# A two-pass graph network kernel: the first stage of 24 of the dense edge groups made in pass 1, kept in a DRAM table and read back in pass 2

## The reference

```python
# layer 0
edge_input = concat([x[src], edge_attr])                 # 96 + 32
messages = gelu(edge_input @ mW1 + mb1) @ mW2 + mb2
gates = sigmoid(gelu(edge_input @ gW1 + gb1) @ gW2 + gb2)
aggregated = segment_sum(messages * gates, dst)
h = x + gelu(concat([x, aggregated]) @ uW1 + ub1) @ uW2 + ub2
x1 = layernorm(x + layernorm(h) * ln_g + ln_b)
# layer 1
deg = segment_sum(ew, dst) + 1
norm = rsqrt(deg)[src] * ew * rsqrt(deg)[dst]
out = layernorm(x1 + segment_sum((x1 @ W)[src] * norm, dst) + self_loop + b)
```

## Time and profile before

| what | value |
|---|---|
| median of 3 runs | 1701.44 us (1701.17 to 1703.01) |
| the profiled execution, its own time | 1702.55 us |
| its span, first to last instruction | 1700.7 us |
| busy: PE, DVE, ACT, POOL | 1373.8, 1113.0, 560.2, 1239.9 us |
| granted TensorE clock, mean | 0.902 |
| DMA, mean | 54 GB/s |

### The profile page before, as it was taken

The page is one execution under the profiler, slowest core; times in us unless marked ns, Lnnn a source line. Parts: engine busy times, 40 slices in busy tenths (PEclk is TensorE's granted clock), DMA queues, the critical chain, the costliest instruction groups (busy, mean ns, idle before and its releaser), DMA issues.

```text
span 1700.7 us, 29806 instructions
## 1 busy us (share of the span) xinstructions
PE 1373.8 (81%) x10228; PEld 1247.9 (73%) x10229; DVE 1113.0 (65%) x3157; ACT 560.2 (33%) x1191; POOL 1239.9 (73%) x1321
## 2 busy tenths in 40 slices
PE   2347888776677777777777775999999999999996
PEld 1337888776677677666767764888888888888885
DVE  5215888766656666666566674686778677768674
ACT  1113544443333333333333330333222233322221
POOL 7777777777777777777777716777777777777774
PEclk8778999889888888988888886999999999999998
DMA  4422222222222222222222201121222121222211
GB/s 111 117 67 55 63 62 59 58 55 58 55 55 55 56 57 56 55 57 55 55 55 55 57 16 39 41 46 43 45 45 45 43 45 43 45 43 46 46 43 35
DMA packets 64801, 91.01 MB, mean 54 GB/s; under 512 B 38429, under 2 KB 39997, under 8 KB 64543
## 3 DMA queue, kind: packets, MB, share of 16 engines
q0 software_dynamic: 41856, 64.37, 17.9%
q10 hardware_dynamic: 11376, 14.90, 3.0%
q1 hardware_dynamic: 11408, 9.71, 2.0%
HBM read 84.07 MB, written 4.82 MB: 52 GB/s over the span
## 4 chain that ended last, share of the span: by engine, by line
POOL 61%; issue 21%; DVE 6%; PE 5%; DMA 3%; DVEq 2%; another core or an unknown queue 1%; ACT 0%; ACTq 0%; POOLq 0%
POOL rows L368 61%; DMA rows<-in_x_nat,idx 3%; PE ps_hid L485 1%; PE ps_bt L611 1%; PE ps_win L431 1%; DVE logit L968 1%; DVE edges L946 1%; DVEq L967 1%; PE ps_xt L460 0%; DVE prod L965 0%; DVEq L893 0%; DVEq L995 0%; DVE root L934 0%; DVE step L930 0%
## 5 line engine op out<-in xcount | busy, mean ns | idle before, releaser
L368 POOL DMA_INDIRECT rows<-in_x_nat,idx x782 | 741.5, 948 | 240.1 <-issue 237.0
L368 POOL DMA_INDIRECT rows<-x1s_table,idx x526 | 496.3, 944 | 204.4 <-issue 160.0
L485 PE MATMUL ps_hid<-w,edges 128*128 128x192 f32 x1568 | 350.1, 350 | 0.0
L460 PE MATMUL ps_xt<-ident,rows 128*96 128x128 f32 x784 | 138.9, 336 | 235.0 <-DMA rows<-in_x_nat,idx 234.8
L485 PEld LDWEIGHTS ps_hid<-w,edges 128*128 128x128 f32 x1568 | 296.8, 209 | 11.6 <-issue 1.0
L460 PEld LDWEIGHTS ps_xt<-ident,rows 128*96 128x96 f32 x784 | 107.0, 154 | 249.9 <-DMA rows<-in_x_nat,idx 247.1
L611 PE MATMUL ps_bt<-x_nat,wide 128*96 128x96 f32 x3136 | 273.8, 249 | 0.0
L611 PEld LDWEIGHTS ps_bt<-x_nat,wide 128*96 128x96 f32 x3136 | 270.8, 166 | 0.0
L670 ACT ACTIVATE edges<-ps_hid 128x384 f32<-128x384 f32 x392 | 192.2, 490 | 234.2 <-PE ps_hid L485 222.2
L656 ACT ACTIVATE edges<-ps_xt 96x512 f32<-96x512 f32 x196 | 109.9, 589 | 352.9 <-PE ps_xt L460 352.4
L431 PEld LDWEIGHTS ps_win<-hot,edges 128*98 128x98 f32 x1568 | 175.5, 190 | 28.1 <-DVE edges L946 25.5
(11 more groups left out here) (137 smaller groups left out, 1543.9 us busy)
## 6 DMA issues: line engine op xcount, KB each, us to landing
rows<-in_x_nat,idx POOLq DMA_INDIRECT x782, 2.5
edges<-in_edge_t ACTq DMA_DIRECT2D x96, 128.0 KB, 2.4
rows<-x1s_table,idx POOLq DMA_INDIRECT x526, 2.5
wide<-in_x_t SPq DMA_DIRECT2D x1, 2376.5 KB
out_nodes<-y SPq DMA_DIRECT2D x49, 48.0 KB
x1s_table<-x_nat ACTq DMA_DIRECT2D x47, 48.0 KB
dst_rows<-in_dst_rows SPq DMA_DIRECT2D x1, 392.0 KB
dst_i<-in_dst_t SPq DMA_DIRECT2D x1, 392.0 KB, 4.0
```

The costliest lines, as they stand in the source:

```text
L368: nc.gpsimd.indirect_dma_start(out=rows[slot][:, k, :], out_offset=None, in_=table, in_offset=bass.IndirectOffsetOnAxis(ap=idx[:, TG * g + ...
L460: mm = nc.tensor.transpose(ps_xt[m // 4][0:ND, P * (m % 4):P * (m % 4 + 1)], rows[v][:, m, :], ident[:, :])
L485: mm = nc.tensor.matmul(ps_hid[j % 2][:, HC * q:HC * (q + 1)], feat[u][:, P * m:P * (m + 1)], w1[:, :], start=False, stop=(q == 1))
```

## The change

A row is now 12 groups, with dense groups at places 0, 3, 5, 8 and 10: 40 dense and 58 gathered. Of five dense groups two (B) are made as before, 16 in all; three (P), 24 in all, have their first stage made in pass 1: 96 pairs of tiles, one pair in each step from group 2 on. A step of pass 1 now begins on PE with one tile of the pair, in `ps_xt`, and ends with the other, in `ps_hid`; in between, the first layer is made in two halves of four tiles that take both banks of `ps_hid`, the transposes stand after the first half, and ACT's Gelus and copies are twice as wide and half as many. DVE makes the one-hots of the next step's pair after the node block and ahead of the logit. ACT copies the cells, and SP writes them, 614 KB a pair, into `b_table`. In pass 2 SP reads the table of a P group, 2.46 MB, into the buffer of its parity when the group two before it has been summed. A P group's sums are made transposed ([96, 96] with `x_nat` as weights), copied and turned by PE (`turn_over`). Several small buffers share one tile now.

```diff
+ROW = 12
+STARTS = (0, 3, 5, 8, 10)
+KINDS = "BPBPP"
+PAIR_AT = 2
+TURN_AFTER, PLACE_AFTER, SUMS_AFTER = 5, 11, 32
 # sync
+            def load(d):
+                if d < NTURN and KIND[d] == "P":
+                    p = STORED.index(d)
+                    sp.dma_start(unit_b[d % 2], b_table[P * p:P * (p + 1), :]).then_inc(s_loaded[d % 2], 16)
             def end1():
+                for n in range(PAIRS):
+                    p, v = n // (TG // 2), n % (TG // 2)
+                    sp.wait_ge(s_pair_out, 2 * n + 2)
+                    sp.dma_start(b_table[...], ready_b[n % 2]).then_inc(s_stored[n % 2], 16)
...
+                for q in range(NTURN):
+                    sp.wait_ge(s_rowsum, q + 1)
+                    load(q + 2)
+                    outputs(q)
 # tensor, step1
+                building = easy and g >= PAIR_AT
+                if building:
+                    pair_cells(g - PAIR_AT, 0, g)
+                for half in range(2):
+                    if half == 0:
+                        if building and g > PAIR_AT:
+                            pe.wait_ge(s_pair_out, 2 * (g - PAIR_AT))
...
+                    wait(pe, s_gelu, 2 * g + half)
+                    for j in range(2):
+                        nc.tensor.matmul(ps_hid[j][:, 0:2 * HC], ones_b[:, :], flat(b1_split[:, :, :]), start=True, stop=False)
+                        for q in range(2):
...
                     mm.then_inc(s_pre, 1)
+                    if half == late and not (isinstance(g, int) and g == NG - 1):
+                        if building:
+                            pe.wait_ge(s_pair_out, 2 * (g - PAIR_AT) + 1)
+                        transposes(k + (v + 1) // SLOTS, (v + 1) % SLOTS)
+                    for also in beside[2 * half:2 * half + 2]:
...
+                if building:
+                    pair_cells(g - PAIR_AT, 1, g)
+            def pair_cells(n, i, g):
+                if i == 0:
+                    pe.wait_ge(s_pair_hot, n + 1)
+                    pe.wait_ge(s_feat, g + 1)
+                else:
+                    pe.wait_ge(s_gelu, 2 * g + 2)
+                for m in range(2):
+                    mm = nc.tensor.matmul(ps_pair[i][:, m, 0:HW], pair_low[n % 2][:, i, :], pair_place[n % 2][:, 2 * i + m, :], ...)
+                mm.then_inc(s_pair_cells, 1)
 # tensor, pass 2, a P group
+                        dense_sums(q, range(0, TURN_AFTER))
+                        turn_over(q - 1)
+                        dense_sums(q, range(TURN_AFTER, PLACE_AFTER))
                         place_sums(q - 1)
+                        dense_sums(q, range(PLACE_AFTER, SUMS_AFTER))
+                        gathered_of(turn)
+                        outputs(q - 1)
+                        dense_sums(q, range(SUMS_AFTER, NB))
 # scalar, step1
+                if building:
+                    pair_copy(g - PAIR_AT, 0)
+                for half in range(2):
+                    act.wait_ge(s_pre, 2 * g + half + 1)
+                    nc.scalar.activation(<four tiles of hid>, ps_pair[1][:, :, 0:2 * HC], ACT.Gelu).then_inc(s_gelu, 1)
+                    if half == late and not (isinstance(g, int) and g == NG - 1):
+                        copy_rows(g + 1, 1 - u)
+                    if half == (0 if isinstance(g, int) and g == NG - 1 else u) and not (isinstance(g, int) and g == 0):
                         squash1(g - 1, 1 - u)
...
+                if building:
+                    pair_copy(g - PAIR_AT, 1)
 # vector, step1
                 if b is not None and not (isinstance(b, int) and b == NB - LAST):
                     block1a(b)
-
-                dve.wait_ge(s_gelu, 4 * g + 4)
+                if easy and PAIR_AT <= g + 1 < NG:
+                    pair_hot(g + 1 - PAIR_AT)
+
+                dve.wait_ge(s_gelu, 2 * g + 2)
 # vector, pass 2
-                    if q + 1 < NTURN:
+                    if q + 1 < NTURN and KIND[q + 1] == "B":
                         for m in range(2):
                             dense2(q + 1, m)
```

More of the change, by code:

```diff
@@ L26 @@
 REST = NT - -(-E // P)
-SQUASH_AFTER = (0, 3)
 WD = 12
@@ L43, in second_pass @@
 def second_pass():
-    turns = [[TURN * q + 1, TURN * q + 2, TURN * q] for q in range(NTURN)] + [list(range(MIXED, NG))]
+    ends = DENSE[1:] + [MIXED]
+    turns = [[g for g in range(d + 1, e)] + [d] for d, e in zip(DENSE, ends)] + [list(range(MIXED, NG))]
     order = [g for turn in turns for g in turn]
@@ L89, in gnn_kernel @@
         w1 = sb("w1", [P, HC])
[L90 to L93, removed]
+        b1, b1_rest, b1_part, b1_sum = [shared[0:3, GE + 2 * HC * i:GE + 2 * HC * (i + 1)].rearrange("p (k c) -> p k c", k=2)
+                                        for i in range(4)]
         b1_hi = sb("b1_hi", [3, 2, HC], bf16)
@@ L352, in end1 @@
                     sp.dma_start(x1s_view[:, NB - LAST + m, :], x_nat[:, NB - LAST + m, :]).then_inc(s_xsw, 16)
[L353 to L356, removed]
+                for q in range(NTURN):
+                    sp.wait_ge(s_rowsum, q + 1)
+                    load(q + 2)
+                    outputs(q)
+                outputs(NTURN)
             sp.wait_ge(s_steer, 1)
@@ L467, in step1 @@
                     transposes(0, 0)
[L468 to L473, removed]
+                beside = spaced([] if b is None else [None, lambda: block1b(b)] if u == 0 else
+                                [lambda: agg(b, 1, 2 * b + 3, b - 2), None, lambda: upd_in(b, 1, *place(b)), lambda: upd_out(b, 1, place(b)[0])])
+                building = easy and g >= PAIR_AT
[5 more added lines that the diff above has]
+                            pe.wait_ge(s_pair_out, 2 * (g - PAIR_AT))
                         if isinstance(g, int) and g == 0:
@@ L477, in step1 @@
                         pe.wait_ge(s_edge[u], 16 * (SLOTS // 2 * k + v // 2 + 1))
[L478 to L486, removed]
@@ L487, in step1 @@
-                    mm.then_inc(s_pre, 1)
-                    if also is not None:
-                        also()
-                    if u == 0 and j == 0 and not (isinstance(g, int) and g == 0):
+                        pe.wait_ge(s_feat, g + 1)
[3 more added lines that the diff above has]
+                        for q in range(2):
+                            m = 4 * half + 2 * j + q
+                            mm = nc.tensor.matmul(ps_hid[j][:, HC * q:HC * (q + 1)], feat[u][:, P * m:P * (m + 1)], w1[:, :],
+                                                  start=False, stop=(q == 1))
@@ L606, in dense_sums @@
                     pe.wait_ge(s_xs, NB)
                     pe.wait_ge(s_xstc, NB)
-                wait(pe, s_rowsumc, d)
-                pe.wait_ge(s_cellc, TG * (d + 1))
-                for c in range(NB):
-                    mm = nc.tensor.matmul(ps_bt[0:TW, 0:ND], wide[:, TW * c:TW * (c + 1)],
-                                          x_nat[:, c, :], start=(c == 0), stop=(c == NB - 1))
-                mm.then_inc(s_rowsum, 1)
+                if chunks[0] == 0:
+                    wait(pe, s_rowsumc, d - 1)
+                    if KIND[d] == "B":
+                        wait(pe, s_rowsumc, d)
+                        pe.wait_ge(s_cellc, TG * (BUILT.index(d) + 1))
+                    else:
+                        pe.wait_ge(s_loaded[d % 2], 16 * sum(e % 2 == d % 2 for e in STORED if e <= d))
@@ new lines, in dense_sums @@
+                for c in chunks:
+                    if KIND[d] == "B":
+                        mm = nc.tensor.matmul(ps_bt[0:TW, 0:ND], unit_b[d % 2][:, TW * c:TW * (c + 1)], x_nat[:, c, :],
+                                              start=(c == 0), stop=(c == NB - 1))
+                    else:
+                        mm = nc.tensor.matmul(raw_sums(d), x_nat[:, c, :],
+                                              unit_b[d % 2].rearrange("p (k x) -> p k x", k=TG)[:, :, WD * c:WD * (c + 1)],
+                                              start=(c == 0), stop=(c == NB - 1))
```

271 lines of the change are left out of this document (180 added, 91 removed).

## The result

| | before | after |
|---|---|---|
| median of 4 runs | 1701.78 us (1701.17 to 1703.01) | 2102.8 us (2100.55 to 2104.53) |
| profiled execution: its time, its span | 1702.55, 1700.7 | 2101.7, 2099.9 |
| granted clock, mean | 0.902 | 0.882 |

The changed kernel is slower, ratio 1.2354, 95% interval 1.2339 to 1.237. The forecast was 2095 us.

What follows compares the result with a forecast made beforehand. A serial loop through PE, ACT and DVE bounds pass 1, no longer POOL: pass 1 to 1386.6, plus 30.7 between passes, 8 rows of 81 and 28.7 outside them, 2094.0 of span, 2095 us; range for all 1930 to 2170.

Steps and rivals of the forecast that it cites:

- The loop: Pass 1: PE's every step must go through DVE before the next; 25.3 us a pair at full clock against POOL's 20.0.
- The four legs: Pass 1, one pair: PE and ACT even step 5.2, DVE even 10.1, PE and ACT odd 6.8, DVE odd 3.2 us.
- leg 3: Pass 1, odd step on PE and ACT, cells to squash with hand-overs: 6.8 us at full clock.
- The rival that POOL still sets pass 1: Pass 1 ends as before and the change is faster: 1629 us, or 1709 with pass 2's waits; chance 0.07.
- the slack of 6.3 us: Pass 1: time the other engines have spare under POOL's 20.0 us for two groups, from a catching-up pace of 13.7.
- 1.7 us a pair: Pass 1: slow-clock cost on leg 3's cells and first half, bounds 0 and 2.25; makes a pair 27.0 us.
- The rival without the slow clock: The loop bites in pass 1 without the slow clock: 78 us less, 2017; chance 0.17 shared with pass 2 without waits.
- a pass 2 without waits: Pass 2 rows lack the new waits: 80 us less, 2015; with no slow clock too, 1937; shared chance 0.17.
- The first full loop: Start of pass 1: group 5's late loads and slow half bring the loop's beginning to 142.7 us.
- the pricing of the writes: Pass 1 table writes: about 5 us with landing, two steps (27 us) allowed before ACT waits, so cost nothing.
- The wait before the second B: Pass 2, each row: one-hots behind layer norm make PE wait 6 us, then work about 1.5 us longer at slow clock.
- The second wait: Pass 2, each row: the last P group's 2.46 MB load takes 13.1 us with landing, so PE waits 2.5.

Runs made afterwards that it cites:

- hot_first: Against the changed kernel, DVE makes the pair's one-hots first in its step, ahead of the gate; 1701.07 us, ratio 0.9993 to the kernel before.
- early_dense: Against the changed kernel, pass 2 only: DVE makes the next B group's one-hots right after the present one's cells; 2036.98 us, ratio 1.1967 to the kernel before.
- hot_before_block: Against the changed kernel, DVE makes the pair's one-hots ahead of the node block in even steps; 1942.13 us, ratio 1.1412 to the kernel before.

## Why the prediction was right, point by point

**The loop.** The four legs were to take 5.2, 10.1, 8.5 (6.8 and the slow clock's 1.7) and 3.2 us; they took 5.1, 10.3, 8.6 and 3.2. Over all 46 pairs it is (1404.26 - 1.9 - 154.3) / 46 = 27.1, against 27.0 (with the 1.9 us that the prediction takes from the last loop to the last window). That it is the loop, not the work in it, is shown from two sides: without PE's wait 302 of the 401 us went, and with DVE's one-hots ahead of the gate all but 7 us of the loss of pass 1. DVE's waits for squash were to be 3 us in each step and are 3.2 in the even one and 5.1 to 5.4 in the odd one, which is leg 3 less DVE's work beside it. The rival that POOL still sets pass 1 was right in its premise, that DVE's work fits (19 by my sum; 18.4 us a pair as its own pace in hot_first, 16.5 of them busy), and needed the order that hot_first has: its 1709 us with the waits of pass 2 left in is near the 1701.07 of that run. One reading was off without weight for the sum: the slack of 6.3 us rests on one fast pair, 13.7 us; five pairs on end took 15.0, so it was 5.0.

**The clock.** 1.7 us a pair was a choice between 0 and 2.25. The stretch behind the wait ran at 0.60, leg 3 was 1.8 longer than its full-clock 6.8, and filling the wait gave back 1.4 to 1.6 a pair on two other chips. The rival without the slow clock, 2017, falls, and so does that of a pass 2 without waits, 2015, as a row took 79.4 and not 71.

**The start, mis-sized.** The first full loop was to begin at 142.7 and began at 154.3, 11.6 late. I had priced the writes at nothing for two steps' cover, 27 us. In the loop that held, by the list of DMA issues (count, size of one, us to landing, as the earlier trace rows):

```profile
b_table<-shared SPq DMA_DIRECT2D x96, 600.0 KB, 3.4
```

But the first write, issued at 81.03 amid the first loads, was not there until ACT had waited 38.7 us, to 135.13. PE stood in the step of group 4 all that time, and `agg` of group 5 began at 147.81, where it had begun at 134.97 before the change. The step that failed is the pricing of the writes: I looked at their cover in the loop and not at the start. This is read from the trace; no run leaves the first write out.

**The turn between the passes.** The last window came at 1404.26 instead of 1386.6: 11.6 from the start, and 46 x 0.13 = 6 from the legs. From there to the cells behind the output blocks it was 29.1, predicted 30.7. (The prediction calls these the first cells of pass 2, but four tiles are made ahead of the blocks in both kernels, here from 1411.58.)

**The rows of pass 2.** Predicted 81 us, measured 79.4. The wait before the second B was to be 6 us and was 5.2 to 6.5. The slow work behind it, 1.5 us by the prediction, was some 2: the cells of three tiles from 1638.33 on took 5.3 us, where those from 1299.69 on took 3.3 in the kernel before. early_dense removed both and 8.2 us a row. The second wait did not come: 2.5 us a row for the load were predicted, 20 us in all, and PE waited 0.5 us in all. I had taken 265 GB/s from the first loads; with the table's load the engines moved 336, 436 and 368 GB/s, gathers included, in three 2 us stretches, and the 2.46 MB, issued at 1660.03, were there before 1670.4. Whether the larger pieces of the table make the difference, no run tests. Here the page that I had weighed and set aside, the Trainium skill's "DMA: Bandwidth & Descriptors", section "Specifications", was nearer with its 358 GB/s than my row, though two of the three stretches are above it. The other terms of a row came to 71.2 us (79.4 less the 8.2 of early_dense), predicted 70.9.

**The sum.** 2094.0 + 17.7 (last window) - 1.6 (between the passes) - 8 x 1.6 (rows) + 2.8 (outside the rows, 31.5 against 28.7) = 2100.1; the span was 2099.9. That 2095 came so near is in part luck, as 17.7 and 12.8 have opposite signs.

**The expectations that missed.** For hot_before_block I followed only PE's wait and not the logit behind the block: I redrew one edge of the loop and did not walk round it again. For hot_first, 1765 to 1795, I took POOL's 20.0 us for the least that a pair can take, though the rows of up to 8 groups lay ready when the others came out of the start; at 18.4 us a pair, 46 pairs end 46 x 1.6 = 74 us sooner than that, and 2102.8 - 46 x 7.1 - 74 is 1702.

## What to carry to other kernels

When idle time on one engine is to be filled, a sum per engine says only that the work fits; put each new hand-over into every engine's written order, and walk round once from it to itself. If the walk is longer than the present pace, that is the new pace: a walk of 25.3 us at full clock against a pace of 20.0, and 1.7 of slow clock on top, cost 327 of 401 us here, with PE, the busiest engine of pass 1, at 73%. Most of the rest was lost because a slower loop can't catch up after a late start, as the kernel before did at 15.0 us a pair. Look then for a place in the queue where the new work waits for nothing of its own step: two lines moved brought the kernel back to its time before (ratio 0.9993), and the same look at pass 2 saved 66 us by itself. And price a hidden transfer at the start of a stage too, where the queue is full of the first loads.

## What the runs showed that I had not expected

- A write of 600 KB to DRAM landed 3.4 us after its issue in the steady loop, and 54.0 us after it while the first loads ran.
- Work that computes nothing made the kernel faster: thirty matmuls a pair, 64 and 72 us on two chips, with the mean clock at 0.96 instead of 0.83 on the third.
- An engine that sets the average pace doesn't set every pair's: POOL needs 20.0 us for two groups, yet the others ran at 15.0 and 18.4 us a pair for hundreds of us, on rows gathered while they stood still.
- Two chips ran the same kernel before in 2609 to 2614 us, where a third took 1702 us, with equal instruction durations and pauses between PE's matmuls. early_dense was at a ratio of 1.1967 on the first chip, and the same kernel with 23 copies more at 0.993 on the others: a ratio from one chip says little of another where what bounds the kernel differs.
